# A decoder layer on one core: the last step and tail of cross-attention in another order, with both quarters' token rows stored ahead of the last expert weights

## The reference, cut to what matters

```
x = layernorm(x + self_attention(x))                     # 32 heads of 16, causal
x = layernorm(x + cross_attention(x, ctx_4096, mask))    # 32 query heads of 128, 8 key/value heads, rotary
x = layernorm(x + experts(x))                            # 16 experts, 4 per token, and one shared expert
# cross_attention: q = rope(x @ wq), k = rope(ctx @ wk), v = ctx @ wv
#   w = softmax(where(mask, q.k / sqrt(128), -1e9));  out = (w @ v) @ wo
# experts: scores = sigmoid(x @ gate_w.T) + bias; the top 4 are weighted by score / sum
#   out = sum_e weight_e * (silu(x @ Wg_e) * (x @ Wu_e)) @ Wd_e + (silu(x @ Sg) * (x @ Su)) @ Sd
```

## Time and profile before

| | us |
|---|---|
| three runs, median (lowest, highest) | 1825.41 (1824.2, 1831.57) |
| the profiled execution | 1826.89 |
| its span, first to last instruction | 1825.1 |
| PE busy in the span | 1718.2 (94%) |
| DVE busy | 1333.3 (73%) |
| ACT busy | 924.3 (51%) |
| POOL busy | 895.3 (49%) |
| mean granted clock of TensorE | 0.977 of 2.4 GHz |

### The profile page before, as it was taken

One profiled execution on the slowest core, in us unless ns is written; L12 is line 12 of the kernel. 1 busy time (PEld: TensorE's weight loads), 2 busy tenths in 40 slices (PEclk: granted clock), 3 DMA queues, 4 the chain that ended last, 5 costly groups with the idle time before them and its releaser, 6 DMA issues. The chain is left out here.

```text
span 1825.1 us, 39045 instructions
## 1 busy us (share of the span) xinstructions
PE 1718.2 (94%) x15412; PEld 994.3 (54%) x15412; DVE 1333.3 (73%) x2260; ACT 924.3 (51%) x1548; POOL 895.3 (49%) x732
## 2 busy tenths in 40 slices
PE   6999999899999999999999999999798999999990
PEld 4667676555555555555555555555454555455550
DVE  5787789688888888888888888888788444344445
ACT  4566666665546464555555554556531333333335
POOL 6643122464646455546555464646341455455550
PEclk9999999899999999999999999999899999999995
DMA  8711010221413222213122131212135678787668
GB/s 241 179 40 28 8 61 3 91 67 41 139 42 116 74 71 95 86 60 126 70 70 93 36 106 57 93 47 71 54 133 162 152 151 219 192 231 152 118 103 294
DMA packets 84946, 190.41 MB, mean 104 GB/s; under 512 B 10848, under 2 KB 29664, under 8 KB 82720
## 3 DMA queue, kind: packets, MB, share of 16 engines
q1 hardware_dynamic: 61680, 129.55, 21.0%
q0 software_dynamic: 23088, 58.37, 15.7%
HBM read 124.68 MB, written 63.21 MB: 103 GB/s over the span
## 5 line engine op out<-in xcount | busy, mean ns | idle before, releaser
L288 PE MATMUL bank<-xhl,front_h 128*128 128x512 f16 x704 | 267.8, 380 | 15.5 <-DVEq L68 13.8
L290 PE MATMUL bank<-xhl,front_l 128*128 128x512 f16 x704 | 267.8, 380 | 0.0
L289 PE MATMUL bank<-xhl,front_h 128*128 128x512 f16 x704 | 267.8, 380 | 0.0
L1000 POOL TENSOR_TENSOR xa_xs<-xa_xs,sn 128x512 f32<-128x512 f32 x160 | 233.9, 1462 | 45.8 <-ACT xa_xs L1047 45.8
L1011 POOL TENSOR_TENSOR xa_sc<-xa_sc,xa_rs 128x1024 f32<-128x1024 f32 x32 | 62.3, 1945 | 382.1 <-DVE xa_rs L1241 382.1
L1005 POOL TENSOR_TENSOR xa_rr<-xa_x,xa_xs 128x512 f32<-128x512 f32 x160 | 231.9, 1450 | 12.7 <-DVE xa_x L1147 0.2
L288 PE MATMUL bank<-out_h,xa_oh 128*128 128x512 f16 x512 | 194.1, 379 | 9.4 <-DVE xa_ol L1132 6.6
L1881 POOL DMA_INDIRECT scratch_y<-raw_front,moe_to x79 | 125.3, 1586 | 149.7 <-DVE mo_zl L1934 116.5
L290 PE MATMUL bank<-out_h,xa_ol 128*128 128x512 f16 x512 | 194.0, 379 | 0.0
L289 PE MATMUL bank<-out_l,xa_oh 128*128 128x512 f16 x512 | 194.0, 379 | 0.0
L1046 ACT ACTIVATE xa_xs<-bank 64x512 f32<-64x512 f32 x160 | 95.1, 594 | 131.6 <-PE bank L290 127.9
(11 more groups left out here) (299 smaller groups left out, 4763.9 us busy)
## 6 DMA issues: line engine op xcount, KB each, us to landing
xa_rawc<-in_ew SPq DMA_DIRECT2D x32, 768.0 KB, 5.6
moe_ring<-scratch_w SPq DMA_DIRECT2D x16, 1536.0 KB, 8.4
scratch_w<-xa_chunk_h SPq DMA_DIRECT2D x32, 384.0 KB, 2.3
scratch_w<-xa_chunk_l SPq DMA_DIRECT2D x32, 384.0 KB, 3.3
raw_front<-in_xwq SPq DMA_DIRECT2D x8, 1024.0 KB, 7.7
raw_out<-in_xwo SPq DMA_DIRECT2D x8, 1024.0 KB, 5.3
scratch_y<-xa_zero SPq DMA_DIRECT2D x18, 256.0 KB, 5.9
acc<-in_x POOLq DMA_DIRECT2D x4, 1024.0 KB, 13.1
```

The costliest lines, as they stand in the source:

```text
L288: pe.matmul(out_ap, ah, bh, start=start and m == 0, stop=False)
L289: pe.matmul(out_ap, ah, bl, start=False, stop=False)
L290: mm = pe.matmul(out_ap, al, bh, start=False, stop=stop and m == n - 1)
L1000: PO.mark(pool.tensor_tensor(xr, xr, sn[:, :].rearrange("p (a s) -> p a s", a=1) .to_broadcast([P, QT // S, S]), ALU.mult), f"sm{r}", st)
```

## The change

Nothing is computed otherwise, and no instruction is added or dropped. Six things stand elsewhere:

- In step (7, 3) DVE no longer waits for and makes the low part of the shared expert's weights (`wfl`, L983) between the additions of `w0` and `w1`. It is made in the tail, between the last additions of `w0` and `w1`.
- In step (7, 3) the four low parts of quarter 0 (L262) are parted: two before the addition of `w2`, two behind the reciprocal.
- The last `chunk_h` (ACT) goes from behind the exponentials of (7, 3) to behind the tail's `back_p` copies; the last `chunk_l` (DVE) to behind the tail's `back_lo` and aggregate. They get semaphores of their own.
- The tail's statistics of quarter 2 go behind `back_p_lo`, the low parts of quarter 1 and `back_lo`.
- SP stores the rows of quarters 0 and 1 first, each once POOL has made it, and the last chunk afterwards.
- The counters are filled so that the numbers others wait for stay in order (`also`): the event `wfl` of (7, 3) is now counted with `w0`, `cl` with `w3`, and `ch` with `ex1`.

```diff
@@ SP
-                            sp.wait_ge(DV.sem, DV.value("cl", Step(i, q)))
-                            met(sp)
+                            if (i, q) == (NG - 1, NQ - 1):
+                                for c in range(2):
+                                    rows = xs_rows[c * QT:(c + 1) * QT, :].rearrange("(t p) n -> p t n", p=P)
+                                    after.wait(sp, after.PO, f"lo{c}.3")
+                                    sp.dma_start(rows[:, :, 0:D], rows_h).then_inc(s_xr, 16)
+                                    sp.dma_start(rows[:, :, D:2 * D], rows_l).then_inc(s_xr, 16)
+                                sp.wait_ge(s_last_l, 1)
+                            else:
+                                sp.wait_ge(DV.sem, DV.value("cl", Step(i, q)))
+                                met(sp)
                             store_chunk(i, q)
...
-                    for c in range(2):
-                        rows = xs_rows[c * QT:(c + 1) * QT, :].rearrange("(t p) n -> p t n", p=P)
-                        after.wait(sp, after.PO, f"lo{c}.3")
-                        sp.dma_start(rows[:, :, 0:D], rows_h).then_inc(s_xr, 16)
-                        sp.dma_start(rows[:, :, D:2 * D], rows_l).then_inc(s_xr, 16)
@@ ACT, step and tail
-                        act.wait_ge(s_cr, i * (16 * NQ) + 16 * (q + 1))
-                        act.wait_ge(s_cw, i * (32 * NQ) + 32 * (q + 1))
-                        AC.mark(act.activation(chunk_h[:, :], rawc[:, :], ACT.Copy, scale=WS), "ch", st)
+                        if (i, q) != (NG - 1, NQ - 1):
+                            AC.mark(chunk_hi(i, q), "ch", st)
...
                     back_p(Step(None, 0))
+                    chunk_hi(NG - 1, NQ - 1).then_inc(s_last_h, 1)
                     back_o(Step(None, 0), range(4))
@@ DVE, step
-                            back_add(st, [0])
-                        if q == 3:
+                            back_add(st, [0], ("wfl",) if (i, q) == (NG - 1, NQ - 1) else ())
+                        if q == 3 and i < NG - 1:
                             dve.wait_ge(AC.sem, AC.value("wfh", st))
                             DV.mark(split_front_lo(dve, i), "wfl", st)
...
@@ DVE, tail
-                    dve.wait_ge(DV.sem, DV.value("w3", st, 1))
-                    after.statistics(dve, 2, range(TQ))
                     back_p_lo(st)
                     for t in range(TQ):
                         after.low(dve, 1, t, bank[(2, 3, 0, 1)[t]])
+                    back_lo(st, range(4))
+                    dve.wait_ge(DV.sem, DV.value("w3", st, 1))
+                    after.statistics(dve, 2, range(TQ))
                     after.aggregate(dve, 2)
-                    back_lo(st, range(4))
+                    dve.wait_ge(s_last_h, 1)
+                    chunk_lo().then_inc(s_last_l, 1)
...
                     back_add(st, [0])
                     after.inverse(dve, 2, 1)
+                    dve.wait_ge(AC.sem, AC.value("wfh", Step(NG - 1, NQ - 1)))
+                    split_front_lo(dve, NG - 1)
                     back_add(st, [1, 2, 3])
```

More of the change, by code:

```diff
@@ L864, in cross_attention @@
                 s_cr, s_cw, s_xr = sem("xa_s_cr"), sem("xa_s_cw"), sem("xa_s_xr")
+                s_last_h, s_last_l = sem("xa_last_h"), sem("xa_last_l")
                 zero, s_zero, s_zeros = b("zero", [P, D]), sem("xa_zero"), sem("xa_zeros")
@@ L1023, in _, with chunk_hi @@
                     AC.start(act)
+                    def chunk_hi(i, q):
+                        act.wait_ge(s_cr, i * (16 * NQ) + 16 * (q + 1))
+                        act.wait_ge(s_cw, i * (32 * NQ) + 32 * (q + 1))
+                        return act.activation(chunk_h[:, :], rawc[:, :], ACT.Copy, scale=WS)
                     def back_p(st):
@@ L1098, in step @@
                             s2 = sc[:, h, :, :, :].rearrange("p a b c -> p (a b c)")
-                            AC.mark(act.activation(s2, s2, ACT.Exp, scale=float(HD2) ** -0.5), f"ex{h}", st)
-                        act.wait_ge(s_cr, i * (16 * NQ) + 16 * (q + 1))
-                        act.wait_ge(s_cw, i * (32 * NQ) + 32 * (q + 1))
-                        AC.mark(act.activation(chunk_h[:, :], rawc[:, :], ACT.Copy, scale=WS), "ch", st)
+                            AC.mark(act.activation(s2, s2, ACT.Exp, scale=float(HD2) ** -0.5), f"ex{h}", st,
+                                    ("ch",) if (i, q, h) == (NG - 1, NQ - 1, 1) else ())
+                        if (i, q) != (NG - 1, NQ - 1):
+                            AC.mark(chunk_hi(i, q), "ch", st)
                         if i == NG - 1 and q >= 2:
@@ L1133, in back_lo, with chunk_lo, back_add @@
                                                       heads(oh, tp, b2), ALU.subtract), f"lo{c}", st)
-                    def back_add(st, ts=range(TQ)):
+                    def chunk_lo():
+                        return dve.scalar_tensor_tensor(chunk_l[:, :], rawc[:, :], WS, chunk_h[:, :], ALU.mult, ALU.subtract)
+                    def back_add(st, ts=range(TQ), also=()):
                         for t in ts:
@@ L1139, in back_add @@
                             DV.mark(dve.scalar_tensor_tensor(row, home[f"w{t}"][:, :], 1 / (WS * OS), row,
-                                                             ALU.mult, ALU.add), f"w{t}", st)
+                                                             ALU.mult, ALU.add), f"w{t}", st, also)
                     def cosine(st, r, also=()):
@@ L1231, in step @@
                             after.inverse(dve, q - 2, 1)
-                        if i == NG - 1 and q == 3:
-                            for t in range(TQ):
+                        last = (i, q) == (NG - 1, NQ - 1)
+                        if last:
+                            for t in range(2):
                                 after.low(dve, 0, t, bank[4 + t])
@@ L1241, in step @@
                         DV.mark(dve.reciprocal(rs[:, :, :], sm[:, :, :]), "rc", st, ("w3",) if alone else ())
+                        if last:
+                            for t in range(2, TQ):
+                                after.low(dve, 0, t, bank[4 + t])
                         if not alone:
-                            back_add(st, [3])
-                        dve.wait_ge(AC.sem, AC.value("ch", st))
-                        DV.mark(dve.scalar_tensor_tensor(chunk_l[:, :], rawc[:, :], WS, chunk_h[:, :], ALU.mult, ALU.subtract), "cl", st)
+                            back_add(st, [3], ("cl",) if last else ())
+                        if not last:
+                            dve.wait_ge(AC.sem, AC.value("ch", st))
+                            DV.mark(chunk_lo(), "cl", st)
                     for i in range(NG):
@@ L2153, in build @@
             ln2 = NormSteps("ln2", numbered("st", 0) + ["ag0", "iv0", "sh0"] + numbered("st", 1) + ["ag1", "iv1", "sh1"] + numbered("lo", 0)
-                            + numbered("st", 2) + numbered("lo", 1) + ["ag2", "iv2", "sh2"] + numbered("st", 3) + ["ag3", "lo2.0", "iv3", "sh3"]
+                            + numbered("lo", 1) + numbered("st", 2) + ["ag2", "iv2", "sh2"] + numbered("st", 3) + ["ag3", "lo2.0", "iv3", "sh3"]
                             + numbered("lo", 2, (1, 2, 3)) + numbered("lo", 3),
```

## The result

| | before | after |
|---|---|---|
| median of five runs, us | 1825.41 (1821.97 to 1831.57) | 1817.51 (1814.09 to 1819.48) |
| the profiled execution: time, span | 1826.89, 1825.1 | 1817.68, 1815.9 |
| next stage's first matmul, us of the span | 1326.28 | 1317.38 |

The medians differ by 7.90 us, a ratio of 0.9957. The ratio after/before that was put on record from the runs is 0.9947, interval 0.9926 to 0.9968: faster, and clear of no change; whether by more than the 0.5% that the prediction called the limit, this interval leaves open. A second comparison gave 0.9965 (0.9953 to 0.9978), 6.4 us. The forecast of 1821 was too high, and the prediction had put 0.89 on a change within 0.5% and only 0.06 on faster.

The account below looks back on a forecast made before the run. DVE's order, behind PE's waits, bounds the stage end. Projection 7.8 us earlier, 2.7 given back: 5.1 gained, giving 1821.8 against the profiled execution or 1820.3 against the median; forecast 1821, range 1816 to 1827.

Parts of the forecast that it names:

- the limit: Whole-kernel time: a difference of 0.5%, 9.1 us, is about what a measurement can tell from no change.
- the debt: Tail: moved DVE work delays additions; PE waits 2.0 us before `w2`, 0.6 before `w3`; 2.7 of 7.8 us given back.
- how the numbers follow: Step from the 5.1 us gain to chances: 0.89 same within 0.5%, 0.06 faster, 0.05 slower.
- I take 1305.9: Tail: output projection starts at 1305.9, between 1305.4 and 1306.4 for PE's two clocks, 7.8 us earlier than 1313.69.
- Gate 1.03: Tail, DVE: the gate after the chunk takes 1.03 us, from 1311.4 to 1312.4, before `w0`'s addition.
- Rival B: Output projection: the new 2.0 us PE stall halves the clock for `w2`, `w3` and transposes; 1828.7, slower; chance 0.08.
- Rival A: Last step and tail: slow chunk low part or late `Exp`; gain 3.7 us, both 2.3; 1823 to 1824.5; chance 0.15.
- a slow chunk: Tail, DVE: the chunk's low part takes about 3.13 us even without POOL beside it, 1.4 us less gain.
- a hole ahead of `Exp`: Last step, ACT: a drain at the table switch starts `Exp` 1.4 us later; gain 3.7 us.
- Rival D: Tail: additions are less late than thought and the wait for them isn't paid; 1817 to 1818.5; chance 0.06.
- the SP order: Stage end: SP is only 0.8 us ahead of PE, so both must move; POOL's 8.70 us store wait goes.
- SP's 5 us to spare: Stage end: SP's last chunk store lands at 1315.5, 5 us before it would hold the barrier.

Follow-up runs that it names:

- second comparison: Kernel before and changed kernel measured again without any edit: ratio 0.9965 (0.9953 to 0.9978).
- the fed runs: Changed kernel plus twelve PE matmuls whose results nobody reads: ratio 0.9955 alone; 0.9954 with DVE's tail additions of `w0` and `w1` also placed earlier.
- the undone order: Changed kernel with SP's store order put back, last chunk first, then both quarters' rows: ratio 1.0044 (1.0031 to 1.0056), stretch 66.55 us.
- Store order alone: Kernel before with only SP's order changed, rows of quarters 0 and 1 before the last chunk: ratio 1.0001 (0.9992 to 1.0009), stretch 60.85 us.

## Why the prediction was wrong

Its mechanism held, in nearly every place: the chain it named is the one that got shorter. What failed is the size of the gain, by terms of the sum that were too dear, and the step from the gain to the chances:

- **The step "how the numbers follow".** The sum was a gain of 5.1 us, 0.3%, and I put 0.89 on "within 0.5%" with 0.06 left for faster. The gain in the stretch is 6.36 us: 54.50 in both profiles of the changed kernel, 60.85 or 60.86 in three of four of the kernel before. Of the 8.2 us by which the projection came earlier, the debt took back 1.9, where I had 2.7 of 7.8. On top of it the first comparison had its differences between executions, 2.5 us in the two profiles, and the kernel before is longer by itself at times: 62.84 in one of the four. With 6.4 us as the centre, 9.1 is no far tail, and 0.06 was too little. Nor was 0.5% the limit: the second interval, 0.9953 to 0.9978, tells 0.35% from nothing.
- **"I take 1305.9", the middle of two clocks.** PE's transposes and `back_pv` ran at full clock in both profiles (eight transposes in 1.04 us, against 1.73); the projection started at 1305.45 in the old frame. 0.45 us too little gain.
- **"Gate 1.03".** I took the duration from a place where POOL was at work beside it, though for the chunk, a few lines ahead, I had taken that apart. Here, without POOL, it took 0.36, to the start of the addition. 0.67 us too little gain. The rest, 0.14, is spread over the order.
- **The debt** was said to be 2.0 and 0.6 us; it is 1.46 and 0.41 at full clock, mostly because the gate was dear in my sum.
- **Rival B** was half right: the clock did fall, in one of the two profiles, but earlier than I had it, in `w0`, ahead of the debt and so not because of it; the fed runs point to the sparse work before it (PE waited 1.70 us for `xa_ptl` and 2.15 us before the projection). There it costs 1.69 us of matmul time and nothing in the end, as DVE is the later one. Rival A's two prices (a slow chunk, a hole ahead of `Exp`) are both refuted by the rows above: 1.73 us, and 0.02 us after the table load.
- **Rival D** had the measured 1817.51 in its range (1817 to 1818.5), but not for its reason: the debt was paid, and the number came from a gain of 6.4 and differences between executions. The forecast range of 1816 to 1827 held the result in the same way, near its edge.

What the prediction had right: `nm` 5.8 us earlier (forecast 5.7), before which ACT's table load had become the bound (reciprocal at 1296.55 in the old frame, forecast 1296.6); `back_pv` at 1301.82 (1301.8); the SP order as the condition for the rest, which the undone order shows; the wait for the additions; SP's 5 us to spare.

The Trainium skill, "TensorE: Matmul & The Clock Gate", section "What's actually happening", has the lower clock as the default that activity lifts. The profiles here agree as far as they go. Fed, the projection never ran below full clock (three profiles); unfed it did in five of eleven. Over the last 45 us of the stage it is none of three against ten of eleven. The feeding was tried in no other way, and three profiles are few.

## What to carry to other kernels

When work is moved off one chain, write down what it now stands ahead of, and look for a second loss beside it: here a wait for DVE and a fallen clock covered each other, so that removing one gave 0.2 us at most while the other was there, and removing both gave 1.8. Stores that free a buffer go ahead of stores that nobody waits for, above all once the rest is faster. And for small changes compare a stretch that begins at an untouched landmark: two profiles of the changed kernel agreed in it to 0.01 us, where their spans lay 1.8 apart. Look at the clock in it all the same: one of four profiles of the kernel before was 2.0 us longer.

## What the runs showed of the hardware that I had not expected

- The granted clock in the same place of the same kernel differs between executions: the 12 matmuls of `w0` took 2.59 us in three profiles of the kernel before and 4.56 in a fourth.
- The start of the program, up to 120 us, varied by 5.7 us over 14 profiles of kernels that are alike there.
- DVE's operations on SBUF alone took longer beside a busy POOL. The gate's low part, 64 columns, took 0.52 to 0.55 us in the five profiles where POOL was at work throughout it, and 0.22 to 0.23 in the nine where it was not. The chunk's 1536 columns took 3.13 us in the six profiles where `nm` was at work during the first 1.52 us, and 1.72 to 1.75 in the other eight. "Store order alone" comes near to a trial of it: DVE's stream is that of the kernel before, only POOL's rows lie elsewhere, and the gate's two operations took 0.18 and 0.23 us, while the chunk, still beside `nm`, took 3.13.
- The time to landing of the same store in the same place of the queue differs: the last part of quarter 0's rows, behind the chunk's two stores, took 7.02 us with the order undone, and 5.3 to 5.7 in the five profiles of kernels whose order was never changed. Why is open.
